# Two small PSUM banks for the shared pieces of an attention loop, three for its scores, and two moved steps

## The reference

```python
q = (x @ Wq + bq).reshape(b, s, H, dh)      # H = 16 heads of dh = 8
k = (x @ Wk + bk).reshape(b, s, H, dh)
v = (x @ Wv + bv).reshape(b, s, H, dh)
scores = jnp.einsum('bqhd,bkhd->bhqk', q, k) / math.sqrt(dh)
attn = jax.nn.softmax(scores, axis=-1)
out = jnp.einsum('bhqk,bkhd->bqhd', attn, v).reshape(b, s, d)
return out @ Wo + bo
...
x = x + _layernorm(_attention(...), ln1_g, ln1_b)
```

## Time and profile before

| | |
|---|---|
| median of 3 runs | 5303.79 us (5299.88 to 5307.32) |
| the profiled execution | 5306.9 us, span of its instructions 5305.2 us |
| PE, weight load, DVE, ACT, POOL busy | 74%, 52%, 67%, 45%, 45% of the span |
| mean granted TensorE clock | 0.897 |
| DMA queue q1 | 17.5% of 16 engines' span |

### The profile page before, as it was taken

How to read it: one execution, slowest core, us unless ns; L and a number is a source line. 1 busy time by engine, 2 the same in 40 slices (tenths; PEclk the granted TensorE clock), 3 DMA queues, 4 the chain that set the end, 5 groups by cost and what they waited for, 6 DMA issues and landing times. The chain is left out here.

```text
span 5305.2 us, 89506 instructions
## 1 busy us (share of the span) xinstructions
PE 3913.4 (74%) x25840; PEld 2745.5 (52%) x25840; DVE 3560.2 (67%) x9744; ACT 2366.2 (45%) x5537; POOL 2394.7 (45%) x3900
## 2 busy tenths in 40 slices
PE   5889786679999787558868826457786887787364
PEld 3666464556666465446646526422333664455263
DVE  5787675656666675656657757669997664676566
ACT  2444464255555465234435514345552553355142
POOL 3656442433343442446633244367775661232542
PEclk9999898889999899789979959879998999899597
DMA  5000232100000232133313211212222330232112
GB/s 218 0 0 0 95 115 80 43 24 1 1 0 1 81 115 77 38 114 108 104 70 108 90 38 40 64 48 62 64 64 69 111 106 1 87 107 72 41 40 74
DMA packets 243672, 341.35 MB, mean 64 GB/s; under 512 B 26848, under 2 KB 185968, under 8 KB 242224
## 3 DMA queue, kind: packets, MB, share of 16 engines
q1 hardware_dynamic: 230064, 309.19, 17.5%
q0 software_dynamic: 13184, 27.22, 1.5%
HBM read 182.77 MB, written 147.26 MB: 62 GB/s over the span
## 5 line engine op out<-in xcount | busy, mean ns | idle before, releaser
L507 DVE TENSOR_REDUCE l0att_rowmax<-l0att_S 128x2 f32<-128x512 f32 x512 | 339.7, 686 | 144.7 <-PE l0att_S L678 143.7
L507 DVE TENSOR_REDUCE l1ffn_rowmax<-l1ffn_S 128x2 f32<-128x512 f32 x512 | 340.9, 686 | 134.5 <-PE l1ffn_S L678 133.1
L869 POOL TENSOR_TENSOR wb_prob<-wb_prob,wb_rden 128x128 f32<-128x128 f32 (+1 forms) x512 | 248.9, 508 | 378.3 <-DVE wb_rden L1046 378.0
L1397 POOL DMA_INDIRECT results<-e_y,e_back x220 | 216.1, 982 | 417.0 <-DVE e_y L1628 398.2
L1943 POOL TENSOR_TENSOR ssm_hc<-core_AW_all,ssm_Cs 128x512 f32<-128x512 f32 x256 | 321.2, 1271 | 129.6 <-DVE core_AW_all L2089 96.5
L911 ACT ACTIVATE wb_prob<-wb_biased,wb_nmax 128x128 f32<-128x128 f32 (+1 forms) x512 | 228.6, 447 | 254.2 <-DVE wb_nmax L1039 251.3
L2188 PE MATMUL ssm_Y<-ssm_hc,core_ident 128*128 128x512 f32 x512 | 290.8, 679 | 56.0 <-POOL ssm_hc L1943 29.8
L678 PE MATMUL l1ffn_S<-l1ffn_K,l1ffn_Q 128*128 128x512 f32 x512 | 253.5, 499 | 96.2 <-DVE l1ffn_rowmax L507 58.7
L2089 DVE TENSOR_TENSOR_SCAN core_AW_all<-core_AW_all,ssm_U 128x512 f32<-128x512 f32 x256 | 310.2, 1212 | 1.4 <-ACT core_AW_all L2032 1.4
L678 PE MATMUL l0att_S<-l0att_K,l0att_Q 128*128 128x512 f32 x512 | 249.3, 490 | 59.7 <-DMA l0att_K<-bounce 52.1
L2032 ACT ACTIVATE core_AW_all<-ssm_dt,ssm_A 128x510 f32<-128x510 f32 x256 | 178.5, 716 | 221.6 <-DVE core_AW_all L2089 220.0
(11 more groups left out here) (499 smaller groups left out, 11841.5 us busy)
## 6 DMA issues: line engine op xcount, KB each, us to landing
bounce<-l0att_parts SPq DMA_DIRECT2D x128, 256.0 KB, 2.8
bounce<-l1ffn_parts SPq DMA_DIRECT2D x128, 256.0 KB, 2.8
ssm_Cs<-c_rows SPq DMA_DIRECT2D x128, 256.0 KB
routed<-core_Y SPq DMA_DIRECT2D x8, 2048.0 KB, 23.5
l0att_Q<-bounce SPq DMA_DIRECT2D x128, 128.0 KB
l0att_K<-bounce SPq DMA_DIRECT2D x128, 128.0 KB
bounce<-l1att_parts SPq DMA_DIRECT2D x64, 256.0 KB, 2.8
l1ffn_Q<-bounce SPq DMA_DIRECT2D x128, 128.0 KB
```

The lines of the kernel that those rows point to most:

```text
L507: dve.tensor_reduce(out=rowmax[:, jp, qt, 2 * pair:2 * pair + 2], in_=S[a % 2][:].rearrange("p (j k) -> p j k", j=2)[:, :, 0:keys(qt)], op ...
L869: ins = pool.tensor_tensor(out=prob[:, w_ % 4, a:b], in0=prob[:, w_ % 4, a:b], in1=rden[:, w_ % 4, n:n + 1].to_broadcast([P, b - a]), op=A ...
L1397: pool.indirect_dma_start(core.results, bass.IndirectOffsetOnAxis(ap=back[:, j % RING, 1:2], axis=0), y[:, j % RING, :], None).then_inc(y_ ...
```

## The change

The T banks become three, used in turn over the whole run and not by slot; the shared pieces get two banks, `F0` and `F1`, by the parity of their running number, with a semaphore for each. A piece now waits for the piece two before it. Three waits that the single bank implied are written out: `qk` for `h`, `on` for `n0` and `n1`, `out` for `on`. On SP, `store(r + 2)` moves to the head of the list of a round where r is 0 or more. `finish_norm` moves from slot 14 of the round in which its sequence's `out` is made to slot 2 of the next round, and once more behind the last round.

```diff
-        T = [ps(f"T{b}") for b in range(4)]
+        T = [ps(f"T{b}") for b in range(3)]
         O = ps("O")
-        F = ps("F")
+        banks = [ps("F0"), ps("F1")]
...
+        def bank(x, n):
+            return banks[turn_of[x, n] % 2]
+
+        def gone(x, n):
+
+            return f_taken[turn_of[x, n] % 2].sem
+
+        def out_of(eng, x, n):
+
+            eng.wait_ge(gone(x, n), turn_of[x, n] // 2 + 1)
...
             for r in ROUNDS:
+                if inside(r + 2) and r >= 0:
+                    store(r + 2)
                 if inside(r + 1):
                     send(r + 1, 1)
                 if inside(r):
                     send_max(r, 1)
                 if inside(r + 2):
-                    store(r + 2)
+                    if r < 0:
+                        store(r + 2)
                     send(r + 2, 0)
...
-                                       T[u % 4][:].rearrange("p (j q) -> p j q", j=2)[:, :, q0:L], ACT.Exp)\
+                                       T[(r * UNITS + u) % 3][:].rearrange("p (j q) -> p j q", j=2)[:, :, q0:L], ACT.Exp)\
...
-                    if u == 14 and out_norm and inside(r - 1):
-                        finish_norm(r - 1)
+                    if u == 2 and out_norm and inside(r - 2):
+                        finish_norm(r - 2)
+            if out_norm:
+                finish_norm(SEQS - 1)
...
             def claim(x, n):
-                await_(pe, f_taken, turn_of[x, n])
+                if turn_of[x, n] >= 2:
+                    pe.wait_ge(gone(x, n), turn_of[x, n] // 2)
...
-                    pe.wait_ge(f_taken.sem, turn_of["h", n] + 1)
+                    out_of(pe, "h", n)
...
                 elif x == "on":
+                    for t in range(QT):
+                        out_of(pe, f"n{t}", n)
                     claim(x, n)
...
                 elif x == "out":
+                    out_of(pe, "on", n)
                     claim(x, n)
...
-                await_(pe, exped, exped.at(n, u - 3))
-                bank = T[u % 4]
+                await_(pe, exped, exped.at(n, u - 2))
+                bank = T[(n * UNITS + u) % 3]
```

More of the change, by code:

```diff
@@ L353, in part @@
                     for x in range(2):
-                        pool.wait_ge(f_taken.sem, turn_of["qk"[x] * 2, n] + 1)
+                        out_of(pool, "qk"[x] * 2, n)
                         own.step(pool.tensor_tensor(out=full[:, x, :], in0=rt[:, x, 0, :], in1=rt[:, x, 1, :],
@@ L358, in part @@
                 else:
-                    pool.wait_ge(f_taken.sem, turn_of["qk", n] + 1)
+                    out_of(pool, "qk", n)
                 await_(pool, stored, stored.at(n - 1, 64))
@@ L447, in after_slot @@
                 if x:
+                    F = bank(x, n)
                     if x == "h":
@@ L452, in after_slot @@
                             act.activation(hT[:], F[:, 0:L], ACT.Identity, scale=affine[0], bias=affine[1])\
-                                .then_inc(f_taken.sem, 1)
+                                .then_inc(gone(x, n), 1)
                         else:
-                            act.activation(hT[:], F[:, 0:L], ACT.Copy).then_inc(f_taken.sem, 1)
+                            act.activation(hT[:], F[:, 0:L], ACT.Copy).then_inc(gone(x, n), 1)
                         if n < 2:
@@ L463, in after_slot @@
                         act.wait_ge(max_copied.sem, max_copied.at(n, jp + 1))
-                        act.sem_inc(f_taken.sem, 1)
+                        act.sem_inc(gone(x, n), 1)
                     elif x == "on":
@@ L467, in after_slot @@
                         await_(act, f_made, turn_of["out", n - 1] + 1 if n else 0)
-                        act.activation(onT[:], F[:, 0:L], ACT.Copy).then_inc(f_taken.sem, 1)
+                        act.activation(onT[:], F[:, 0:L], ACT.Copy).then_inc(gone(x, n), 1)
                 for jp, at in ((1, 3), (0, 13)):
@@ L536, in after_slot @@
                                                                op0=ALU.mult, op1=ALU.mult)
-                        ins.then_inc(f_taken.sem, 1)
+                        ins.then_inc(gone(x, n), 1)
                     elif x == "v":
@@ L545, in after_slot @@
                                               in1=bv[:].rearrange("p (h d) -> p h d", h=H)[:, None]
-                                              .to_broadcast([P, QT, H, DH]), op=ALU.add).then_inc(f_taken.sem, 1)
+                                              .to_broadcast([P, QT, H, DH]), op=ALU.add).then_inc(gone(x, n), 1)
                         else:
-                            dve.tensor_copy(dst, got).then_inc(f_taken.sem, 1)
+                            dve.tensor_copy(dst, got).then_inc(gone(x, n), 1)
                     elif x in ("n0", "n1"):
@@ L562, in finish_out @@
             def finish_out(n):
-                got = F[:, 0:L].rearrange("p (t d) -> p t d", t=QT)
+                got = bank("out", n)[:, 0:L].rearrange("p (t d) -> p t d", t=QT)
                 dve.wait_ge(f_made.sem, turn_of["out", n] + 1)
@@ L569, in finish_out @@
                         dve.wait_ge(advanced.sem, advanced.at(n))
-                    dve.tensor_tensor(out=onto, in0=got, in1=onto, op=ALU.add).then_inc(f_taken.sem, 1)
+                    dve.tensor_tensor(out=onto, in0=got, in1=onto, op=ALU.add).then_inc(gone("out", n), 1)
                     return
                 dve.tensor_tensor(out=fin[:], in0=got, in1=w["bo"][:, None, :].to_broadcast([P, QT, D]),
-                                  op=ALU.add).then_inc(f_taken.sem, 1)
-                dve.wait_ge(f_taken.sem, turn_of["out", n] + 1)
+                                  op=ALU.add).then_inc(gone("out", n), 1)
+                out_of(dve, "out", n)
                 for t in range(QT):
```

4 lines of the change are left out of this document (2 added, 2 removed).

## The result

The changed kernel took 5152.04 us (median of 4 runs, 5149.92 to 5164.97), the one before 5305.56 us (5299.88 to 5312.59) beside it. The ratio is 0.9716, 95% interval 0.9699 to 0.9733. The forecast was 5168 us, range 5120 to 5245.

A forecast was written before the change was run, and what follows sets the result against it. No engine is full; waits between engines ending last on PE set the rounds. Gains of 67 (l1ffn), 46 (l0att), 13.5 (l1att) and 11 us (gqa), 137.5 in all, gave 5166 us, rounded to 5168; range 5120 to 5245.

The forecast's parts named there:

- The norm's move: In l1ffn, the 1.10 us wait ahead of score 1 goes: gain 1.1 us in 16 rounds, 17.6 us per stage.
- the 1.30 us at score 0: In l1ffn, score 0's wait for maximum 14, which stands ahead of the norm; claimed to stay.
- the step that summed it with the rest: Adding the parts' gains: in l1ffn 17.6 + 23.5 - 13 x 0.6 = 33 us per stage; 137.5 us overall.
- The bank waits: PE's waits for bank F ahead of v, n0, n1, h: 1.7 us per full round, 23.5 us per l1ffn stage.
- taken back 0.6 us a round: Deduction in full l1ffn rounds: 0.4 us at score 9 for maximum 7, 0.2 us at n0.
- More comes back: Rival: no DMA delay in l0att, DVE keeps up in l1ffn; about 5138 us, 5120 with the clock; chance 0.17.
- The store in front: In l0att, score 0's K wait goes, score 8 waits about 1 us; 17.4 us rounds, 23 us gained per stage.
- Two terms: In l0att's loop: 8.1 + 0.8 us from score 8 through turn 15 and store; 7.8 us for the send to land.
- the send would wait for the whole store: Rival: the half's data move only after the store's land, score 8 2.4 us later; 5337 us, chance 0.07.
- `l1att`: Bank waits between weigh and kk come out of the round: 13.5 us gained in the stage, rounds of 19.6 us.
- the term of 1.0 us a round: In l1att, the gain from removed bank waits, taken in 12 rounds.
- `gqa`: Bank waits come out at 0.8 us in 12 rounds, 1.5 us for the rest: 11 us, rounds of 19.0 us.

The follow-up runs named there:

- experiment 5: Changed kernel with, in stages without rope, half the store issued ahead of send_max(r + 1, 0) and half behind it: 5179.99 us.
- Experiments 3 and 4: Changed kernel with unread products ahead of first weigh (two in l1att, one in gqa): 5136.61 us; changed kernel with POOL's advance behind the next round's masks: 5136.63 us.
- experiment 1: Changed kernel with the store back in its old place behind send_max(r, 1): 5327.46 us, ratio 1.0038.
- experiment 1's second kernel: Changed kernel with finish_norm back in slot 14: 5230.31 us, ratio 0.9847.

## Why the prediction was right, and where not

- **The norm's move** came as worked out: no wait at score 1, the 1.30 us at score 0 kept, 34 us alone against 35 forecast. But the step that summed it with the rest was wrong: beside two banks and the store's lead it is worth 76 us, since it also keeps the clock.
- **The bank waits.** `v`, `n1` and `h` start 0.24 us behind their turns. `n0` waits 0.14 us for ACT's copy. I had taken back 0.6 us a round in `l1ffn` for DVE in slots 4 to 7, 0.4 of it at score 9; score 9 waits 0 to 0.3 us there. `l1ffn`'s round came out as forecast at 18.1 to 18.2 us. It gave 40 us a stage and not 33, as the stages before had rounds of 21 to 23 us at a clock under 1.00, the one of the earlier trace rows among them; the changed ones have none after the second. Together the five full rounds of that kind took 9 us more than five of 20.4 us, of a surplus of 14 us in the two stages. I had this as a part of the rival "More comes back".
- **Three T banks** cost nothing: in the changed kernel no turn of a full round waits for ACT, and alone they measure as no change.
- **The store in front** did what it should at score 0 and delayed the other half as forecast. The wait at score 8 is 0.5 to 1.1 us (forecast about 1), and the round 17.7 us in the middle, not 17.4. Two terms were a little small: from score 8 to the send's first DMA 9.0 us, where 8.1 + 0.8 were taken, and from L298 to score 8 8.0 us (8.15 in the round shown), where 7.8 were taken. In `l1ffn` the send fitted in most rounds, as forecast: score 8 waits by more than 0.05 us in four of 22 full rounds, 0.37 us in the round shown. That the send would wait for the whole store did not happen. The Trainium skill's rule ("DMA: Bandwidth & Descriptors", section "Queues, rings and completion order") has descriptors taken in ring order, which gives the store's data the first place; it adds that a later transfer may finish its write before an earlier one, which the prediction left out. By the trace the store's data cost 0.2 us on 7.8 at most, and not the time to their landing. In experiment 5 a small transfer took over a microsecond longer beside the store's.
- **`l1att`** is the step that failed in size: 13.5 us forecast, 7 measured. The bank waits did come out of the round: the three full rounds at a clock of 1.00 take 19.0 to 19.6 us, where 19.6 were forecast. But eight of eleven ran at 0.92 and took 20.9 us, longer than the 20.6 us before, so that the term of 1.0 us a round measured 0.2. Experiments 3 and 4 give the missing time back by two different ways. **`gqa`**, with a round of 19.0 us as forecast, gained 18 us and not 11. The eleven full rounds gave 9 us, 0.84 us each where 0.8 were taken. The other 9 lie in the start of the stage (2), its first three rounds (3) and its end (4), for which the forecast had 1.5 us in all.
- **Why the forecast of 5168 was near.** Errors of both signs met: `l1att` 6.5 us less, `l1ffn` 14 more, `gqa` 7 more. That the whole came so near is in part luck: the clock gave some 9 us in `l1ffn` and took some 9 in `l1att`, and the sum had neither. (The sum itself gives 5166 us; it was written as 5168.) The price of each part alone was right only before the others were in. Had the change held the banks without the lead, the same method would have forecast a gain where the runs show a loss of 0.4%: it had no term for the clock.

## What to carry to other kernels

Don't leave one long wait when you take out short ones: read the granted clock of single rounds before and after, since a round can grow when its waits are merged, even if they are less in sum. Where the wait can't be moved, products that nobody reads, put into it, test whether the clock is the cause within one run, and may stay as the cure. And price the parts of a change together, by the loop that closes last with all of them in: here the banks were worth nothing in sum until the store left that loop.

## What the runs showed of the hardware

The granted clock falls within rounds whose longest wait of PE is only about 2 us, in a PE busy over 85% of the time: 2.0 to 2.5 us at score 0 (experiment 1: 0.92), 2.12 us ahead of `weigh` (`l1att` after the change: 0.92). In experiment 1's second kernel it is 1.30 us. After the fall, products run at the lower level of the two, 1.2 instead of 2.4 GHz, for a part of the round (1.51 us against 0.86 for the same sixteen), and the round is 1.3 to 1.6 us longer. A mean of 0.92 is such a mixture. The Trainium skill ("TensorE: Matmul & The Clock Gate", section "A second HAM failure mode: psum-queue depth-cycling") tells of a kernel whose short idle times between groups of products make the clock go back and forth. The trace agrees that it does so without a wait much over 2 us, from 1.00 to 0.92 and back between rounds of `l1att`; but here it is the kernels with fewer short waits that lose it more often.

What decides it stays open. The length of the wait alone does not: `l1att` had 2.13 us in rounds at 1.00 before the change, a round that ends in a wait of 1.97 us stayed at 1.00 in experiment 1, and the waits of 1.30 and 1.10 us stood in rounds of 20.4 us at 1.00 before (17 of 22 full rounds) and in rounds of 20.8 to 22.2 us at 0.86 to 0.91 in experiment 1's second kernel (19 of 22 below 1.00). In the first and the last of these it is the kernel with fewer short waits elsewhere that loses the clock. No run here changed the length of a round apart from its waits.
